# One-core decoder kernel: another order for the first batch of its quantized MLP

## The chip, the cores and the metric

The kernel runs on one core of one Trainium2 chip. The metric is the device time of one execution in microseconds. The median of three runs of the kernel before is 1719.95 us (1714.42 to 1724.76). One execution was profiled: it took 1716.46 us, its trace spans 1714.5 us, and every row below is from it.

## The reference, cut to what matters

Two decoder layers act on x of 4 batches x 512 tokens x 512 features. Each layer is self attention, then a second block, then an MLP, each with a layer norm ahead and a residual around it. The change is in the first layer's MLP, two "bit linear" layers with a GELU between:

```python
def bit_linear(x, w, b, dim_in):
    x_norm = simple_rms_norm(x, dim_in)
    x_q = activation_quant(x_norm)                 # round(x * 127 / max|x|), per token
    w_q = weight_quant(w)                          # sign(w) * mean|w|
    return jnp.einsum('bsd,od->bso', x_q, w_q) + b
h = bit_linear(x, w1, b1, DIM)                     # 512 -> 2048
h = jax.nn.gelu(h, approximate=False)
return bit_linear(h, w2, b2, INNER)                # 2048 -> 512
...
x = x + _L0_xattn_ref(_layernorm(x), ...)          # four experts, a token goes to one
x = x + _L0_ffn_ref(_layernorm(x), w1, b1, w2, b2)
x = x + _L1_attn_ref(_layernorm(x), ...)
```

## The kernel before, in words

The program is a row of phases: Start, Attention, Experts, BitMlp, Attention, Attention (cross), Fp8Linear. Each engine runs its own list in order, and a barrier of all five (L154) stands between phases. SP issues the plain DMAs, POOL (GpSimd) the indirect ones.

Experts writes its results, sorted by expert, to `sorted_y` in memory. BitMlp fetches them: POOL issues one indirect DMA (`take_back`, L145) for each tile of 128 tokens, and the DMA adds into `x`. The four tiles of batch 0 have a semaphore each, `gathered_first`; the later batches one each, `gathered`, with all four tiles on it.

BitMlp works on 4 batches of T = 4 tiles. `steps` runs one step for each tile on each engine: batch 0 unrolled with `first=True`, batches 1 and 2 as a loop, batch 3 unrolled, then four steps that drain the pipeline. `has(k)` says whether the tile k steps back exists. What the engines do:

- VectorE (DVE), `dve_step`. It empties the four PSUM banks of a tile's first layer with scale and bias (L2212, "eviction", 4 instructions). For the tile one step back it takes the row maximum of the GELU's result (L2219) and makes the sum-of-squares operand (L2221). POOL raises that to -1/2 (L2285), and five small operations (`row_factors`, L2146 to L2153) give the tile's factors. Once a batch it also prepares the next batch's input: moments (`norm.dve_moments`, L183 to L194), application (L201), row maxima and squares (`dve_input_rows`, L2162 to L2167), and the input factors (`dve_input_factors`, L2146 to L2153 on four columns) behind a power on POOL (L2278).
- ScalarE (ACT), `act_step`. It applies the GELU (L2119), sums the squares (L2122), scales and rounds the tile one step back (L2127), copies turned tiles out of PSUM (L2089), and at step 2 scales the next batch's four input tiles (L2098).
- TensorE (PE), `pe_step`. It multiplies the first layer (L2053, 16 matmuls a tile), turns the tile three steps back (L2061), multiplies the second layer (L2071), and in step 3, in the midst of those, turns the next batch's input (L2034).

Batch 0 has no batch ahead of it in which to prepare its own input. So `dve` starts with `dve_first_moments` (L2179 to L2189) and `dve_first_factors` (L2194 to L2153) for each of its tiles, with a power on POOL between them (L2310). `act` scales each tile (L2098) and copies it once turned (L2089). `pe` turns tile 0, and inside step 0, behind tile 0's matmuls, it turns tiles 1, 2 and 3 (L2034) ahead of step 1:

```python
        if first and i == 0:
            for k in range(1, T):
                self.pe_first_turn(pe, k)
```

The biases `b1` (1024 KB, the same row for every partition) and `b2` (256 KB) are loaded by SP in `BitMlp.sp`, behind the four `gathered_first` waits. DVE waits for them ahead of its first step.

Of the kernel before, what the change touches and what calls it, by code (L numbers as in the profile page):

```python
# [14 lines left out]
P = 128  # L15
NB = 4
S = 512
D = 512
# [1727 lines left out]
class Experts(Phase):  # L1746
# [15 lines left out]
    def __init__(self, m, name, mats, bufs, early):  # L1762
# [5 lines left out]
        self.xs, self.gate, self.a, self.ys = pair(), pair(), pair(), pair()  # L1768
        self.ahl = take(4 * D, F16).rearrange("p (n a d) -> p n a d", n=2, a=2)
        assert m.used <= ARENA - C * INNER  # L1770
        s = self.sem
# [71 lines left out]
    def sp(self, sp):  # L1843
        self.steps(self.sp_step, sp)
        for k in range(2):
            sp.wait_ge(*self.at(self.sign_done[k], SIGN_PARTS))
            sp.wait_ge(*self.at(self.abs_done[k], SIGN_PARTS))
        self.sp_following(sp)

# [90 lines left out]
class BitMlp(Phase):  # L1940
# [15 lines left out]
    def __init__(self, m, name):  # L1956
        super().__init__(m, name)
        take = m.take
        self.b1, self.b2 = take(INNER), take(D)
        self.h = take(4 * INNER).rearrange("p (n f) -> p n f", n=4)  # L1960
# [10 lines left out]
        self.squares, self.roots = (take(2 * T).rearrange("p (t k) -> p t k", k=2) for _ in range(2))  # L1971
        self.averager = self.junk[:, 0:P]
        assert m.used <= ARENA - C * INNER
        self.signs = m.signs
# [24 lines left out]
    def sp(self, sp):  # L1999
        io, m = self.io, self.m  # L2000
        row = lambda a, n: a.rearrange("(a n) -> a n", a=1).broadcast_to([P, n])

        for t in range(T):
            sp.wait_ge(m.gathered_first[t], 16)
        sp.dma_start(self.b1, row(io["L0_ffn_b1"], INNER)).then_inc(self.const, 16)
        sp.dma_start(self.b2, row(io["L0_ffn_b2"], D)).then_inc(self.const, 16)
        m.wait_back(sp, 1)
        sp.wait_ge(*self.at(self.const, 32))
        self.sp_following(sp)
        self.following.weights.sp_rest(sp)  # L2010

    def steps(self, step, eng):
# [91 lines left out]
    def act_first_turn(self, act, i):  # L2104
        m = self.m
        act.wait_ge(*self.at(self.first_full, i + 1))
        self.act_whole(act, m.xt[:, 0, :, i * P:(i + 1) * P], tile3(m.ps[:, 4 + i, 0:256].bitcast(F16))).then_inc(self.first_free, 1)

    def act_step(self, act, b, i, has, first=False, last=False):
        m = self.m  # L2110
        tile = b * T + i
        if has(3):
            for k in range(2):
                act.wait_ge(*self.at(self.t_full[k], tile - 3 + 1))
                self.act_whole(act, self.q2t[:, (i - 3) % 2, k * 1024:(k + 1) * 1024], m.ps[:, 4 + k, :].bitcast(F16)).then_inc(self.t_free[k], 1)
        if has(0):
            h = self.h[:, i, :]
            act.wait_ge(*self.at(self.bank_free[3], b * (T + 1) + 1 + i))
            act.activation(h, h, ACT.Gelu).then_inc(self.gelu_done, 1)  # L2119
            act.wait_ge(*self.at(self.gelu_done, tile + 1))  # L2120
            act.wait_ge(*self.at(self.ss_done, tile))
            act.activation(self.junk, h, ACT.Square, accum_out=self.ms[:, T + i:T + i + 1]).then_inc(self.ss_done, 1)  # L2122
        if has(1):
            k = (i - 1) % T
            h = self.h[:, k, :]
            act.wait_ge(*self.at(self.factor_chain, tile * self.FACTOR))
            act.activation(h, h, ACT.Identity, scale=self.f[:, T + k:T + k + 1], bias=self.magic).then_inc(self.scaled, 1)  # L2127
        if has(0) and i == 2 and not last:
            self.act_scale_input(act, b + 1)
        if isinstance(b, int) and b == NB and i < self.following.weights.ahead:  # L2130

            self.following.weights.act(act, i)

    def act(self, act):
        act.wait_ge(*self.at(self.consts, 3))
        self.act_first_scale(act, 0)
        for i in range(1, T):
            self.act_first_scale(act, i)
            self.act_first_turn(act, i - 1)
        self.act_first_turn(act, T - 1)  # L2140
        self.steps(self.act_step, act)
# [49 lines left out]
    def dve_first_factors(self, v, ch, i):  # L2191
# [6 lines left out]
        self.row_factors(v, ch, c, D, 0, self.roots[:, i, 1:2], self.alpha1, self.first_factors)  # L2198

    def dve_step(self, v, b, i, has, first=False, last=False):  # L2200
        m = self.m
        tile = b * T + i
        nx = lambda i: slot(m.x, (b + 1) % NB * T + i)
        if has(0):

            for n in range(4):
                v.wait_ge(*self.at(self.bank_full[n], b * (T + 1) + 1 + i))
                if n == 0 and i == 0 and not first:
                    v.wait_ge(*self.at(self.alpha1_ready, b))
                if n == 0 and not first:  # L2210
                    v.wait_ge(*self.at(self.t_full[1], tile - T + 1))
                v.scalar_tensor_tensor(out=self.h[:, i, n * 512:(n + 1) * 512], in0=m.ps[:, n, :], scalar=self.alpha1[:, i:i + 1],  # L2212
                                       in1=self.b1[:, n * 512:(n + 1) * 512], op0=ALU.mult, op1=ALU.add).then_inc(self.bank_free[n], 1)
        if has(1):
# [6 lines left out]
            v.tensor_scalar(self.f[:, col], self.ms[:, col], 1.0 / INNER, 1e-6, ALU.mult, ALU.add).then_inc(self.power2, 1)  # L2221
        if has(0) and i == (1 if first else 0):
            if first:
                m.wait_back(v, 1)
            else:
                m.wait_back(v, 2, 3)
            self.norm.dve_moments(v, b, nx)
# [7 lines left out]
        if has(1):  # L2235
# [3 lines left out]
            ch1.close()  # L2239
        if has(0) and i == 1:  # L2240
            self.norm.dve_apply(v, b, nx, lambda i: m.xn[:, i, :])
            if not last:
                v.wait_ge(*self.at(self.norm.xn_ready, b * T + T))
                self.chi = Chain(self, self.input_chain, self.INPUT, b)
                self.dve_input_rows(v, self.chi, b + 1)
        if has(0) and i == 2 and not last:
            self.dve_input_factors(v, self.chi, b + 1)
# [9 lines left out]
    def dve(self, v):  # L2257
        m = self.m
        ch = Chain(self, self.first_chain, T * self.FIRST, 0)
        self.dve_first_moments(v, ch, 0)  # L2260
        self.dve_first_moments(v, ch, 1)
        v.wait_ge(*self.at(self.abs_all, 1))
        v.tensor_reduce(self.negmean, m.ps[:, 0, 0:2 * SIGN_PARTS].rearrange("p (a n) -> p a n", a=2), AX.X, ALU.add).then_inc(self.mean_done, 1)
        v.wait_ge(*self.at(self.mean_done, 1))
        self.dve_first_factors(v, ch, 0)
        self.dve_first_moments(v, ch, 2)
        self.dve_first_factors(v, ch, 1)
        self.dve_first_moments(v, ch, 3)
        self.dve_first_factors(v, ch, 2)
        self.dve_first_factors(v, ch, 3)  # L2270
        ch.close()
        v.wait_ge(*self.at(self.first_factors, T))
        v.wait_ge(*self.at(self.const, 32))
        self.steps(self.dve_step, v)
# [5 lines left out]
    def pool_step(self, g, b, i, has, first=False, last=False):  # L2280
# [5 lines left out]
        if has(0):  # L2286
            if i == (1 if first else 0):
                self.norm.pool(g, b)
            if i == 1:
                if not last:  # L2290
                    self.pool_root1(g, b + 1)
            xs = slot(m.x, b * T + i)
# [329 lines left out]
```

## Time and profile before

| what | value |
|---|---|
| median of three runs | 1719.95 us |
| the profiled execution | 1716.46 us |
| span of its trace | 1714.5 us |
| TensorE clock granted, mean over the span | 0.958 |
| TensorE matmuls, busy over the span | 1489.2 us (87%) |
| VectorE | 1261.1 us (74%) |
| ScalarE | 871.7 us (51%) |
| GpSimd | 530.4 us (31%) |
| BitMlp, first instruction behind its barrier | 650.79 us |
| next phase, first instruction | 850.90 us |

How to read it: the shares are means over seven phases with different limits, so they say little about BitMlp, which takes 200 us of the 1714.5. There the order of the instructions on each engine and the idle time ahead of single instructions count. The mean clock is close to full speed; single stretches are at half speed.

### The profile page before, as it was taken

The page shows a single profiled execution, that of the slowest core. Times are in us where ns is not written, and L with a number is a line of the kernel's source. Part 1 is how long each engine was busy: PE and PEld are TensorE (multiplying, and loading weights), DVE is VectorE, ACT ScalarE, POOL GpSimd, SP SyncE. Part 2 cuts the span into 40 slices and gives each one's busy share as a digit, 9 for nine tenths or more (in the row PEclk, how much of TensorE's full clock was granted, in tenths as well). Part 3 has the DMA queues.
Part 4 walks back from the last instruction along what each step waited for, and adds up shares of the span by engine and source line. Part 5 has one row for each costly group of instructions (what it writes and reads, how often), then busy time and mean ns, then how long its engine had stood idle before and what let it go on. Part 6 is the DMA issues. An engine that isn't in the chain of part 4 may idle for free. (4 is left out here: it accounts for less than half of the span.)

```text
span 1714.5 us, 26624 instructions
## 1 busy us (share of the span) xinstructions
PE 1489.2 (87%) x8760; PEld 577.9 (34%) x8761; DVE 1261.1 (74%) x1783; ACT 871.7 (51%) x1071; POOL 530.4 (31%) x450
## 2 busy tenths in 40 slices
PE   3789999999959994688798999999999999999948
PEld 1223323233236661344332323333242323323213
DVE  4687897878855556888687788788945776768675
ACT  2245273452822333788737455463837454563735
POOL 1625447355420004422141322323131321414130
PEclk9889999999979997899998999999999999999979
DMA  5241202103313446300230201212031120303002
GB/s 196 74 122 32 68 25 52 47 0 75 119 54 111 147 135 137 54 1 0 62 74 1 54 22 31 84 65 65 25 91 33 45 53 24 73 0 92 12 0 99
DMA packets 82776, 105.40 MB, mean 61 GB/s; under 512 B 14096, under 2 KB 56208, under 8 KB 82576
## 3 DMA queue, kind: packets, MB, share of 16 engines
q1 hardware_dynamic: 79120, 96.10, 19.3%
q0 software_dynamic: 3584, 8.39, 2.3%
q8 instruction: 39, 0.64, 0.2%
q14 instruction: 33, 0.27, 0.1%
HBM read 48.21 MB, written 18.35 MB: 39 GB/s over the span
## 5 line engine op out<-in xcount | busy, mean ns | idle before, releaser
L1224 ACT ACTIVATE arena<-ps 128x1024 f32<-128x1024 f32 x384 | 373.4, 1026 | 108.4 <-PE ps L1075 98.0
L1284 DVE TENSOR_REDUCE arena<-ps 128x2 f32<-128x1024 f32 x256 | 299.7, 1220 | 56.2 <-PE ps L828 56.0
L468 PE MATMUL ps<-xt,w 128*128 128x512 f16 (+1 forms) x1872 | 295.3, 308 | 7.6 <-DVE w L456 3.8
L1075 PE MATMUL ps<-arena 97*128 97x512 f16 (+1 forms) x768 | 211.8, 389 | 14.8 <-ACT arena L1224 10.6
L883 PE MATMUL ps<-arena 128*32 128x512 f32 x1536 | 208.5, 615 | 15.3 <-DVE arena L1319 8.7
L468 PEld LDWEIGHTS ps<-xt,w 128*128 128x128 f16 (+1 forms) x1872 | 151.4, 99 | 141.7 <-issue 36.5
L468 PE MATMUL ps<-w,arena 128*128 128x512 f16 (+1 forms) x804 | 185.5, 381 | 12.7 <-issue 12.7
L1468 DVE TENSOR_TENSOR arena<-arena 128x1024 f32<-128x1024 f32 x128 | 175.2, 1408 | 11.8 <-PE ps L897 9.9
L1725 POOL TENSOR_TENSOR arena<-arena 128x512 f16<-128x512 f32 x96 | 116.6, 1216 | 158.3 <-ACT arena L1204 148.4
L1199 ACT ACTIVATE arena<-ps,arena 128x512 f32<-128x512 f32 x96 | 65.9, 687 | 182.2 <-PE ps L468 171.9
L1581 DVE TENSOR_SCALAR arena<-arena 128x1024 f32<-128x1024 f32 x128 | 106.7, 839 | 68.4 <-ACT arena L1224 67.9
L897 PE MATMUL ps<-arena 128*32 128x512 f32 x1024 | 138.0, 610 | 12.6 <-DVE arena L1468 11.8
L1595 POOL TENSOR_TENSOR arena<-arena 128x512 f16<-128x512 f32 x36 | 56.4, 1566 | 276.5 <-ACT arena L1145 276.5
L1075 PEld LDWEIGHTS ps<-arena 97*128 97x128 f16 (+1 forms) x768 | 59.2, 98 | 198.2 <-issue 100.9
L468 PEld LDWEIGHTS ps<-w,arena 128*128 128x128 f16 x804 | 75.7, 98 | 108.6 <-issue 30.5
L1135 ACT ACTIVATE arena<-ps 128x512 f32<-128x512 f32 x48 | 28.7, 597 | 136.7 <-PE ps L468 136.7
L468 PE MATMUL ps<-w,xt 128*128 128x512 f16 x384 | 92.0, 380 | 0.0
L828 PE MATMUL ps<-arena 32*128 32x512 f16 x512 | 70.0, 394 | 23.9 <-DVE arena L1284 21.7
L2071 PE MATMUL ps<-arena 128*128 128x512 f16 x256 | 63.3, 401 | 27.7 <-ACT arena L2089 27.7
L201 DVE TENSOR_SCALAR xn<-x,mv,rstd 128x512 f32 (+1 forms) x76 | 63.6, 890 | 24.4 <-POOL rstd L214 24.4
L2053 PE MATMUL ps<-arena,xt 128*128 128x512 f16 x256 | 61.9, 399 | 14.1 <-DVE arena L2212 9.4
L211 POOL TENSOR_TENSOR rstd<-mv,eps 128x4 f32<-128x4 f32 x27 | 9.8, 363 | 189.1 <-DVE mv L194 180.1
(217 smaller groups left out, 2001.5 us busy)
## 6 DMA issues: line engine op xcount, KB each, us to landing
arena<-arena SPq DMA_DIRECT2D x576, 64.0 KB, 2.0
raw<-in_ffn_parts SPq DMA_DIRECT2D x16, 512.0 KB, 3.8
raw<-in_ctxT SPq DMA_DIRECT2D x7, 1024.0 KB, 5.2
sorted_x<-arena SPq DMA_DIRECT2D x1, 4864.0 KB, 17.2
arena<-sorted_x SPq DMA_DIRECT2D x19, 256.0 KB, 3.7
sorted_y<-arena SPq DMA_DIRECT2D x19, 256.0 KB, 2.1
out<-x SPq DMA_DIRECT2D x16, 256.0 KB, 2.0
x<-in_x SPq DMA_DIRECT2D x1, 3072.0 KB, 12.0
```

Source lines behind the costliest of these rows:

```text
L201: v.tensor_scalar(dst(i), src(i), m.mv[:, i, 0:1], m.rstd[:, i:i + 1], ALU.subtract, ALU.mult).then_inc(self.xn_ready, 1)
L468: last = pe.matmul(out, left[l](cl[k]), right[r](cr[k]), start=start and k == 0 and a == 0, stop=stop and k == n - 1 and a == 2)
L828: last = pe.matmul(banks[:, k, :], self.qf[rows, 1, 0, g, t * P:(t + 1) * P], self.qf[rows, 0, 0, g, :], start=True, stop=True, tile_posit ...
L883: last = pe.matmul(self.context(g)[HD * j:HD * (j + 1)], self.v[:, kb, HD * (HG * g + j):HD * (HG * g + j + 1)], self.p(u)[:, j * S:(j + 1 ...
L897: last = pe.matmul(self.m.ps[HD * j:HD * (j + 1), 7, :], self.ones, p[:, j * S:(j + 1) * S], start=start, stop=stop, tile_position=(0, HD ...
L1075: last = pe.matmul(self.m.ps[:, j4, :], self.kst[0:R, HG * g + j4, kb * P:(kb + 1) * P], self.qst[0:R, HG * g + j4, :], start=True, stop=True)
L1199: act.activation(self.qb[:, n % 2, :], self.bank(item), ACT.Identity, scale=s, bias=self.pb[:, C * w + c:C * w + c + 1]).then_inc(self.ban ...
L1224: act.activation(self.p(u)[:, 2 * h * S:(2 * h + 2) * S], flat(self.m.ps[:, 2 * h:2 * h + 2, :]), ACT.Exp, scale=SOFTMAX_SCALE).then_inc(s ...
L1284: v.tensor_reduce(self.mx[:, g % 2, j:j + 2, t:t + 1].rearrange("p h t -> p (h t)"), self.slot_banks(item, b), AX.X, ALU.max).then_inc(sel ...
L1468: v.tensor_tensor(self.pair_sum[:, cols], self.p(2 * n)[:, cols], self.p(2 * n + 1)[:, cols], ALU.add).then_inc(self.paired, 1)
L1581: v.tensor_scalar(p, p, slot_col(self.hi, b * T + kb), CLIP_LOW, ALU.min, ALU.max).then_inc(self.clipped[h], 1)
L1725: g.tensor_tensor(self.qf[:, w, 1, c, :], src[:, n % 2, :], self.qf[:, w, 0, c, :], ALU.subtract).then_inc(self.fl, 1)
```

## The change

Four things are altered, all in batch 0 of BitMlp.

1. The loads of `b1` and `b2` move from `BitMlp.sp` to `sp_early`, which SP runs at the end of the Experts phase, behind its last store and ahead of its waits for the signs. The buffers move to the end of BitMlp's space, where Experts has nothing.
2. VectorE's opening is reordered. Tile 0's factors come ahead of tile 1's moments, and tile 0's eviction comes ahead of tile 3's factors. The wait for all four `first_factors` moves behind that eviction.
3. In step 1 the moments of batch 1 come behind tile 0's factors, and the application and the input rows move to step 2, behind tile 1's factors, with the input factors right behind them. POOL's power for them moves to step 2 as well.
4. ScalarE's opening is reordered: scale 0, copy 0, scale 1, scale 2, copy 1, GELU of tile 0, scale 3, copy 2, copy 3. TensorE's list stays as it is.

```diff
@@ Experts.sp
         self.steps(self.sp_step, sp)
+        self.sp_following(sp)
         for k in range(2):
             sp.wait_ge(*self.at(self.sign_done[k], SIGN_PARTS))
             sp.wait_ge(*self.at(self.abs_done[k], SIGN_PARTS))
-        self.sp_following(sp)
@@ BitMlp.sp, sp_early
-        for t in range(T):
-            sp.wait_ge(m.gathered_first[t], 16)
-        sp.dma_start(self.b1, row(io["L0_ffn_b1"], INNER)).then_inc(self.const, 16)
-        sp.dma_start(self.b2, row(io["L0_ffn_b2"], D)).then_inc(self.const, 16)
         m.wait_back(sp, 1)
...
+    def sp_early(self, sp):
+        row = lambda a, n: a.rearrange("(a n) -> a n", a=1).broadcast_to([P, n])
+        sp.dma_start(self.b1, row(self.io["L0_ffn_b1"], INNER)).then_inc(self.const, 16)
+        sp.dma_start(self.b2, row(self.io["L0_ffn_b2"], D)).then_inc(self.const, 16)
@@ act_step
-            act.wait_ge(*self.at(self.bank_free[3], b * (T + 1) + 1 + i))
-            act.activation(h, h, ACT.Gelu).then_inc(self.gelu_done, 1)
+            if not (first and i == 0):
+                self.act_gelu(act, b, i)
@@ act
         self.act_first_scale(act, 0)
-        for i in range(1, T):
-            self.act_first_scale(act, i)
-            self.act_first_turn(act, i - 1)
-        self.act_first_turn(act, T - 1)
+        self.act_first_turn(act, 0)
+        self.act_first_scale(act, 1)
+        self.act_first_scale(act, 2)
+        self.act_first_turn(act, 1)
+        self.act_gelu(act, 0, 0)
+        self.act_first_scale(act, 3)
+        self.act_first_turn(act, 2)
+        self.act_first_turn(act, 3)
@@ dve_step
-        if has(0):
-            for n in range(4):
...
+        if has(0) and not (first and i == 0):
+            self.dve_first_layer(v, b, i, first)
@@ dve_step, between the maximum and the factors of the tile one step back
-        if has(0) and i == (1 if first else 0):
-            if first:
-                m.wait_back(v, 1)
-            else:
-                m.wait_back(v, 2, 3)
+        if has(0) and i == 0 and not first:
+            m.wait_back(v, 2, 3)
             self.norm.dve_moments(v, b, nx)
@@ dve_step, behind those factors
-        if has(0) and i == 1:
+        if first and i == 1:
+            m.wait_back(v, 1)
+            self.norm.dve_moments(v, b, nx)
+        if has(0) and i == (2 if first else 1):
             self.norm.dve_apply(v, b, nx, lambda i: m.xn[:, i, :])
@@ dve
         self.dve_first_moments(v, ch, 0)
-        self.dve_first_moments(v, ch, 1)
...
         self.dve_first_factors(v, ch, 0)
+        self.dve_first_moments(v, ch, 1)
         self.dve_first_moments(v, ch, 2)
         self.dve_first_factors(v, ch, 1)
         self.dve_first_moments(v, ch, 3)
         self.dve_first_factors(v, ch, 2)
+        v.wait_ge(*self.at(self.first_factors, 1))
+        v.wait_ge(*self.at(self.const, 32))
+        self.dve_first_layer(v, 0, 0, True)
         self.dve_first_factors(v, ch, 3)
@@ pool_step
-            if i == 1:
-                if not last:
-                    self.pool_root1(g, b + 1)
+            if i == (2 if first else 1) and not last:
+                self.pool_root1(g, b + 1)
```

## Rows read from the trace of the kernel before

**Rows 1.** Busy time in two stretches: us, PE, PEld, DVE, ACT, POOL, PEclk, DMA.
```profile
656.48:701.71 45.23, 20.71 (x96) 9.11 (x96) 36.75 (x101) 22.47 (x20) 26.80 (x23) 0.70 0.64 139
713.96:754.88 40.92, 34.38 (x209) 18.05 (x208) 36.34 (x75) 34.48 (x28) 9.52 (x11) 0.96 0.05 7
```

**Rows 2.** Who waited for whom, BitMlp: us in total, times, longest us.
```profile
PE ps L2053 <- DVE arena L2212: 9.4, 1, 9.4
```

**Rows 3.** Timeline, tile 0: start us, us, engine, line, [idle before <-releaser].
```profile
656.48 0.69 DVE L2179 BATCH_NORM_STATS2 stats<-x 128x6 f32<-128x512 f32 x1 [10.26 <-DMA x<-sorted_y,place]
658.12 0.73 POOL L2310 TENSOR_TENSOR arena<-arena,mhalf 128x2 f32<-128x2 f32 x1 [3.01 <-DVE arena L2189]
...
660.51 0.55 DVE L2194 TENSOR_SCALAR xn<-x,mv,arena 128x512 f32<-128x512 f32 x1
...
662.80 0.81 ACT L2098 ACTIVATE arena<-xn,arena 128x512 f32<-128x512 f32 x1 [14.32 <-DVE arena L2153]
...
668.23 0.67 ACT L2089 ACTIVATE xt<-ps,arena 128x512 f16<-128x512 f16 x1
...
668.95 5.81 PE L2053 MATMUL ps<-arena,xt 128*128 128x512 f16 x16 [4.68 <-ACT xt L2089]
```

**Rows 4.** Timeline, fetches of tiles 2 and 3.
```profile
659.04 1.57 POOL L145 DMA_INDIRECT x<-sorted_y,place  x1 [0.19 <-issue]
...
661.80 1.60 POOL L145 DMA_INDIRECT x<-sorted_y,place  x1 [0.17 <-issue]
...
663.82 0.69 DVE L2179 BATCH_NORM_STATS2 stats<-x 128x6 f32<-128x512 f32 x1 [1.14 <-DMA x<-sorted_y,place]
```

**Rows 5.** Timeline, first evictions and matmuls of tiles 1 and 2; matmuls after a pause.
```profile
674.16 2.73 DVE L2212 SCALAR_TENSOR_TENSOR arena<-ps,arena 128x512 f32<-128x512 f32 x4 [1.09 <-DMA arena<-in_L_ffn_b]
...
676.70 7.07 PE L2053 MATMUL ps<-arena,xt 128*128 128x512 f16 x32
...
677.77 3.34 DVE L2212 SCALAR_TENSOR_TENSOR arena<-ps,arena 128x512 f32<-128x512 f32 x4 [0.88 <-PE ps L2053]
...
747.62 2.75 PE L2071 MATMUL ps<-arena 128*128 128x512 f16 x8 [3.97 <-ACT arena L2089]
```

**Rows 6.** Timeline, three ScalarE table loads, one with what follows it.
```profile
677.61 1.28 ACT L2119 ACT_TABLE_LOAD   x1
...
507.84 1.28 ACT L1899 ACT_TABLE_LOAD   x1
...
513.23 0.60 ACT L1899 ACTIVATE arena<-ps 128x512 f32<-128x512 f32 x1 [4.10 <-PE ps L468]
...
900.51 1.28 ACT L1224 ACT_TABLE_LOAD   x1 [3.17 <-PE ps L1075]
```

**Rows 7.** Timeline, preparation of batch 1 on VectorE and GpSimd.
```profile
681.03 2.28 DVE L2219 TENSOR_REDUCE arena<-arena 128x1 f32<-128x2048 f32 x1
683.28 2.46 DVE L183 BATCH_NORM_STATS2 stats<-x 128x6 f32<-128x512 f32 x4
...
685.88 0.28 DVE L194 BATCH_NORM_AGGREGATE mv<-stats 128x2 f32<-128x6 f32 x3
...
687.64 1.92 DVE L201 TENSOR_SCALAR xn<-x,mv,rstd 128x512 f32<-128x512 f32 x4 [0.74 <-POOL rstd L214]
...
692.26 2.72 DVE L2212 SCALAR_TENSOR_TENSOR arena<-ps,arena 128x512 f32<-128x512 f32 x4
692.43 1.01 POOL L2278 TENSOR_TENSOR arena<-arena,mhalf 128x4 f32<-128x4 f32 x1 [4.90 <-DVE arena L2167]
```

**Rows 8.** Timeline, tile 1's factors and batch 1's input factors.
```profile
698.94 0.16 DVE L2146 SCALAR_TENSOR_TENSOR arena<-arena 128x1 f32<-128x1 f32 x1 [1.71 <-POOL arena L2285]
...
699.88 1.26 POOL L2296 TENSOR_TENSOR x<-x,arena 128x512 f32<-128x512 f32 x1 [0.97 <-DVE arena L2153]
699.90 1.26 DVE L2148 TENSOR_SCALAR arena<-arena 128x4 f32<-128x4 f32 x1
...
701.54 0.17 DVE L2153 SCALAR_TENSOR_TENSOR arena<-arena 128x4 f32<-128x4 f32 x1
```

More of the change, by code:

```diff
@@ L1769, in __init__ @@
         self.ahl = take(4 * D, F16).rearrange("p (n a d) -> p n a d", n=2, a=2)
+        m.experts_used = m.used
         assert m.used <= ARENA - C * INNER
@@ L1958, in __init__ @@
         take = m.take
-        self.b1, self.b2 = take(INNER), take(D)
         self.h = take(4 * INNER).rearrange("p (n f) -> p n f", n=4)
@@ L1972, in __init__ @@
         self.averager = self.junk[:, 0:P]
+        assert m.used >= m.experts_used
+        self.b1, self.b2 = take(INNER), take(D)
         assert m.used <= ARENA - C * INNER
@@ L2000, in sp @@
         io, m = self.io, self.m
-        row = lambda a, n: a.rearrange("(a n) -> a n", a=1).broadcast_to([P, n])
-        for t in range(T):
-            sp.wait_ge(m.gathered_first[t], 16)
-        sp.dma_start(self.b1, row(io["L0_ffn_b1"], INNER)).then_inc(self.const, 16)
-        sp.dma_start(self.b2, row(io["L0_ffn_b2"], D)).then_inc(self.const, 16)
         m.wait_back(sp, 1)
@@ L2107, in act_first_turn, with act_gelu @@
         self.act_whole(act, m.xt[:, 0, :, i * P:(i + 1) * P], tile3(m.ps[:, 4 + i, 0:256].bitcast(F16))).then_inc(self.first_free, 1)
+    def act_gelu(self, act, b, i):
+        h = self.h[:, i, :]
+        act.wait_ge(*self.at(self.bank_free[3], b * (T + 1) + 1 + i))
+        act.activation(h, h, ACT.Gelu).then_inc(self.gelu_done, 1)
     def act_step(self, act, b, i, has, first=False, last=False):
@@ L2127, in act_step @@
             act.activation(h, h, ACT.Identity, scale=self.f[:, T + k:T + k + 1], bias=self.magic).then_inc(self.scaled, 1)
-        if has(0) and i == 2 and not last:
+        if has(0) and i == (2 if first else 2) and not last:
             self.act_scale_input(act, b + 1)
@@ L2198, in dve_first_factors, with dve_first_layer @@
         self.row_factors(v, ch, c, D, 0, self.roots[:, i, 1:2], self.alpha1, self.first_factors)
+    def dve_first_layer(self, v, b, i, first):
+        m, tile = self.m, b * T + i
+        for n in range(4):
+            v.wait_ge(*self.at(self.bank_full[n], b * (T + 1) + 1 + i))
+            if n == 0 and i == 0 and not first:
+                v.wait_ge(*self.at(self.alpha1_ready, b))
+            if n == 0 and not first:
+                v.wait_ge(*self.at(self.t_full[1], tile - T + 1))
+            v.scalar_tensor_tensor(out=self.h[:, i, n * 512:(n + 1) * 512], in0=m.ps[:, n, :], scalar=self.alpha1[:, i:i + 1],
+                                   in1=self.b1[:, n * 512:(n + 1) * 512], op0=ALU.mult, op1=ALU.add).then_inc(self.bank_free[n], 1)
     def dve_step(self, v, b, i, has, first=False, last=False):
@@ L2203, in dve_step @@
         nx = lambda i: slot(m.x, (b + 1) % NB * T + i)
-        if has(0):
-            for n in range(4):
[L2207 to L2213, printed above, removed]
+        if has(0) and not (first and i == 0):
+            self.dve_first_layer(v, b, i, first)
         if has(1):
@@ L2245, in dve_step @@
                 self.dve_input_rows(v, self.chi, b + 1)
-        if has(0) and i == 2 and not last:
+        if has(0) and i == (2 if first else 2) and not last:
             self.dve_input_factors(v, self.chi, b + 1)
@@ L2272, in dve @@
         v.wait_ge(*self.at(self.first_factors, T))
-        v.wait_ge(*self.at(self.const, 32))
         self.steps(self.dve_step, v)
```

## The prediction

> **What bounds the kernel now.** The change touches only BitMlp, so I first compared two stretches of it by busy time [rows 1]. From one batch's first eviction to the next one's is 40.92 us, and VectorE is busy in 36.34 of them, ScalarE and TensorE in less. VectorE's list sets the pace there, and those batches are left as they are. The other stretch is the opening, from the first moments at 656.48 to the end of batch 1's input factors at 701.71. VectorE is busy in 36.75 of its 45.23 us, so 8.48 us are idle. Next I looked at the waits: TensorE sits 9.4 us for one eviction, tile 2's [rows 2], which VectorE reaches at 692.26 behind the whole norm of batch 1 [rows 7]. That wait looks like the prize. It isn't, unless the instant at which batch 1 can start moves with it. Last I followed the timeline [rows 3 to 8] to that instant. ScalarE scales batch 1's input only when the input factors are done, and its next copies, TensorE's second layer, the turn of batch 1 and batch 1's first matmuls all stand behind that scaling. I call the end of the input factors the gate: 701.54 + 0.17 = 701.71 [rows 8]. By then the evictions of tiles 0 to 2, the factors of tiles 0 and 1 and the whole input of batch 1 are done. In the new order exactly the same work lies ahead of the gate, so the change is worth what the gate moves. It can't gain more than VectorE's idle time of 8.48 us ahead of it, which is just under 0.5% of 1716.46. It can lose without such a limit.
>
> **Opening, tile 0.** Its moments take 656.48 to 658.0 and POOL's power 658.12 to 658.85 [rows 3]. Today tile 1's moments lie between, and the factors start at 660.51. From there to ScalarE's start at 662.80 is 2.3 us, 2.2 of it VectorE's. Moved ahead, they run from 658.95 to 661.1, and VectorE idles 0.7 us for the power. ScalarE scales until 662.05, TensorE turns (0.6), ScalarE copies in 0.67 [rows 3], and tile 0's matmuls start at 663.5, not 668.95: 5.4 us earlier. At the pace of today's row (5.81 us) they end at 669.3. Alone this gains nothing, since VectorE isn't there to evict.
>
> **The fetch of tile 3.** POOL's power for tile 1 now waits for moments that end at 661.1 + 1.55 = 662.65, and POOL's next fetch is queued behind it. The power ends at 663.5 and the fetch starts 0.2 later, at 663.7, not 661.80. A fetch lands 4.8 us behind its start (659.04 to 663.82) [rows 4], so tile 3 is there at 668.5. VectorE has finished tile 2's moments (663.82 + 1.55) and tile 1's factors (2.2) at 667.5 and idles 1.0. Tile 3's moments end at 670.05, tile 2's factors at 672.2. On POOL the two fetches of batch 1 that follow stay where they are, since they were behind tile 2's power.
>
> **Biases.** Tile 0's eviction waited 1.09 us for b1 [rows 5]. With the loads ahead of the barrier that wait goes: eviction 672.3 to 675.0, 1.9 us earlier than today's 674.16 + 2.73. I cost the two loads at nothing in Experts: SP issues them behind its last store, and POOL's first fetch moves no data until well over 1 us behind the barrier. Bounds: below nothing if the fetches run faster without them beside (0.3), and above by the 4.8 of one landing if they held up the first fetch. I take 0, because they are issued before the barrier opens.
>
> **Tile 1's matmuls.** This is the step that costs. TensorE turns tiles 1, 2 and 3 ahead of step 1, and tile 3 needs its scaling, which needs its factors. Those stand behind tile 0's eviction on VectorE: 675.05 to 677.2. On ScalarE the scaling stands behind the GELU as well. That waits for the eviction, until 675.05, and needs a table load of 1.28 us. The load at 507.84 came 5.4 us ahead of its own activation at 513.23, which waited for TensorE, so a load can run under the wait [rows 6]. ScalarE is free from 673.9, so the load ends at 675.2 and the GELU (1.9) at 677.1, just as the factors do. Scaling ends at 678.1, the turn at 678.75, and tile 1's matmuls start at 678.8, today 676.70: 2.1 later. Today they find TensorE at full speed, 7.07 us for two tiles or 3.5 each [rows 5]. In the new order it has done two turns of 0.6 us in the 8.9 us since tile 0. Today 8 matmuls behind a pause of 3.97 us take 2.75 us [rows 5], 0.34 each, near tile 0's 5.81 / 16 = 0.36 and far from 3.5 / 16 = 0.22. So I take tile 0's pace, 5.7 us, with the first four at the lower of the two clock levels, 1.2 GHz, where 512 columns take 0.43 us. The last bank is full at 684.5 and evicted by 685.3; today 677.77 + 3.34 = 681.1. VectorE idles 3.4 us ahead of the first bank and 2.0 between the banks. At full speed tile 1's eviction would end at 683.1.
>
> **Step 1.** Maximum and sum 2.45 [rows 7], to 687.75. Then VectorE idles 0.8 for POOL's power. Today the moments lie under this wait. Factors 0.8 (698.94 to the next chain) [rows 8], to 689.35. Moments of batch 1, 683.28 to 686.16 [rows 7], 2.9, to 692.25. Tile 2's eviction then starts where it does today, at 692.26. All that was saved is gone by here, and today batch 1's normalized input is complete by then.
>
> **Step 2.** Eviction 2.72, to 695.0. Maximum and sum to 697.4. POOL's power stands behind tile 1's bias add and two fetches, as today, where VectorE idles 1.71 and goes on at 698.94 [rows 8]. POOL reaches them 0.2 later, so factors from 699.15 to 700.0. Application and input rows 687.64 to 692.35, 4.7 [rows 7], to 704.7. POOL's power 0.1 + 1.01 [rows 7], to 705.8; today it lies under tile 2's eviction, now VectorE waits for it. Input factors: today 1.9 to 2.0, of which one operation took 1.26 beside POOL's bias add [rows 8]. POOL's next instruction behind the power is again such an add, so I take 2.0; without the collision it is 0.9. The gate is at 707.8, range 706.7 to 707.8, today 701.71: **6.1 us later**.
>
> The same by idle time: the new order leaves VectorE 0.7, 1.1, 1.0, 3.4, 2.0, 0.8, 1.7 and 1.1, in sum 11.8 us, where today's waits were 0.8, 1.1, 1.1, 0.9, 0.6, 0.7 and 1.7, in sum 6.9. These give 4.9; the rest is rounding and the small gaps between dependent operations.
>
> Behind the gate both lists are the same, the lead of tile 0 has been used up, and each batch repeats one period, so I carry the 6.1 to the end.
>
> **A rule of the skill.** Here the table load at 677.61 was followed at once by its activation, and nothing beside its 1.28 us was paid. The Trainium skill, ScalarE: Activation LUTs, What ACT_TABLE_LOAD costs, adds a drain of about 1.38 us to each switch. By that rule the GELU ends 1.4 later and the change loses about 7.5 us. The sum above goes by the row.
>
> **Rivals.** A, the load runs behind the wait: at 900.51 a load came only at the end of an idle time of 3.17 us [rows 6]. Then the GELU ends 1.1 later, scaling and tile 1 with it: +7.2. The order of load and wait decides; the case is within my forecast's range. B, TensorE is at full speed for tile 1: the eviction ends at 683.1, gate at 705.6, +3.9. The turns at 673.3 and 678.2 speak for it, the slow matmuls behind 3.97 us of pause against. C, the change does what it is meant to. The turn of tile 3 doesn't hold tile 1 (its scaling ends by 674.5), so tile 1 is evicted right behind tile 3's factors, 677.2 to 679.95. Then 2.45 + 0.8 + 0.8 + 2.9 for step 1 give 686.9, and 2.7 + 2.45 + 0.8 + 0.8 + 4.7 + 1.1 + 0.9 for step 2 give 700.4: 1.3 us faster. TensorE's list, with three turns ahead of step 1, speaks against it. D, the later batches swallow the delay: VectorE has 4.6 us idle in each [rows 1]. Then 0. Against it: the idle stands at the turn of the batches, inside the chain that starts at the gate. E, the losses add: A, and a first fetch held up by b1's 1 MB for a few us: +9 to +12.
>
> **How the numbers follow.** Forecast with A: +5 to +7.5, chance 0.60. B 0.16, C 0.06, D 0.09, E 0.09. The profiled execution, 1716.46, is 3.5 us below the median, 1719.95. 1716.46 + 6.1 = 1722.6 there, and 1726 on the median. The runs before lie within 5 us of their median, so I give 1717 to 1732: from C to the foot of E, with some of that spread. 0.5% is 8.6 us, about what a measurement of this kernel can tell from no change. The forecast lies below that bound, but 2.5 us more, by E or by the spread, crosses it: slower 0.23. Faster by 8.6 would take all of the idle time: 0.04. The same 0.73.
>
> **What the profile would show.** Tile 0's matmuls at about 663.5; a wait for the fetch of tile 3; no wait for b1; the turn of tile 3 at 678 behind a pause of TensorE; tile 1's matmuls at tile 0's pace; VectorE idle for L2285 twice and for L2278 once; input factors ending at 707.8; the period between batches still 40.9 us. The prediction is wrong if tile 1's matmuls start before 676, or if the end moves otherwise than the gate.

## The result and the profile after

The changed kernel takes 1723.4 us in the median of 20 runs (1716.54 to 1730.38), the kernel before 1716.44 us (20 runs, 1713.13 to 1724.76). The ratio is 1.0039, 95% interval 1.0027 to 1.0050: by the ratio slower by 6.7 us, with 4.6 and 8.6 as its ends (the two medians lie 7.0 apart). That is 0.39%, so it stayed within the 0.5% that the prediction set as the bound to slower, with a chance of 0.73 for staying there. Twenty runs of each tell it from no change all the same. The forecast was 6.1 us slower. Its 1726 stood on the first three runs of before, whose median lay 3.5 us above that of the twenty.

The profiled execution of the changed kernel took 1723.83 us, span 1721.7. Its BitMlp begins 3.8 us later than that of before (654.62 against 650.79), so all that follows is counted from BitMlp's first moments: 656.48 in the kernel before, 660.38 here. Line numbers have moved: L2055 is the first layer (before L2053), L2220 the eviction (L2212), L2158 to L2165 the factors (L2146 to L2153), L2304 and L2297 POOL's powers (L2285, L2278), L2100 the scaling (L2098), L2091 the copy (L2089), L2036 the turn (L2034), L2114 the GELU (L2119), L2206 the first application (L2194), L2191 the first moments (L2179). In the kernels of the experiments the same lines are off by a few again.

Busy time of the changed kernel in two stretches, the opening up to the gate and one batch, with the columns of [rows 1]:

```profile
660.38:710.66 50.28, 23.37 (x96) 10.03 (x96) 36.74 (x101) 22.76 (x20) 26.80 (x23) 0.70 0.50 98
723.14:764.05 40.91, 34.38 (x209) 18.06 (x208) 36.34 (x76) 34.47 (x28) 9.51 (x11) 0.96 0.05 7
```

This is the case in two lines. VectorE is busy for 36.74 us ahead of the gate (the end of batch 1's input factors), 36.75 before, in the same 101 instructions; the stretch is 50.28 us long, not 45.23. All of the 5.05 us is idle time. The later batches are as they were: 40.91 us from eviction to eviction, 36.34 of them busy.

Who waited for whom, where [rows 2] had 9.4 us:

```profile
PE ps L2055 <- DVE arena L2220: 4.7, 1, 4.7
```

TensorE's longest wait in the opening has halved, and the kernel is slower.

The opening of the changed kernel, from its timeline (start us, us, engine, line):

```profile
662.85 0.55 DVE L2206 TENSOR_SCALAR xn<-x,mv,arena 128x512 f32<-128x512 f32 x1 [0.84 <-POOL arena L2328]
...
667.37 6.22 PE L2055 MATMUL ps<-arena,xt 128*128 128x512 f16 x16 [0.78 <-ACT xt L2091]
667.45 1.60 POOL L145 DMA_INDIRECT x<-sorted_y,place  x1 [0.19 <-issue]
...
672.49 0.69 DVE L2191 BATCH_NORM_STATS2 stats<-x 128x6 f32<-128x512 f32 x1 [1.12 <-DMA x<-sorted_y,place]
...
676.10 2.73 DVE L2220 SCALAR_TENSOR_TENSOR arena<-ps,arena 128x512 f32<-128x512 f32 x4
...
677.58 1.28 ACT L2114 ACT_TABLE_LOAD   x1
...
678.88 1.91 ACT L2114 ACTIVATE arena<-arena 128x2048 f32<-128x2048 f32 x1
...
680.92 0.81 ACT L2100 ACTIVATE arena<-xn,arena 128x512 f32<-128x512 f32 x1
...
681.79 0.61 PE L2036 MATMUL ps<-ident,arena 128*128 128x128 f16 x4 [4.13 <-ACT arena L2100]
682.19 9.11 PE L2055 MATMUL ps<-arena,xt 128*128 128x512 f16 x32
...
684.22 0.75 DVE L2220 SCALAR_TENSOR_TENSOR arena<-ps,arena 128x512 f32<-128x512 f32 x1 [3.34 <-PE ps L2055]
...
685.85 0.75 DVE L2220 SCALAR_TENSOR_TENSOR arena<-ps,arena 128x512 f32<-128x512 f32 x1 [0.88 <-PE ps L2055]
687.02 1.61 DVE L2220 SCALAR_TENSOR_TENSOR arena<-ps,arena 128x512 f32<-128x512 f32 x2 [0.42 <-PE ps L2055]
```

Tile 0's matmuls start 6.99 us behind the first moments (12.47 before), and its eviction at 15.72 without a wait for b1 (17.68 before). Then TensorE pauses 4.13 us for the scaling of tile 3, turns that tile, and only then starts tile 1, at 21.81 (20.22 before). VectorE waits 3.34 us for the first bank and ends the eviction at 28.25 (24.63 before).

The clock at tile 1, changed kernel first, then the kernel before (same columns):

```profile
682.19:685.70 3.51, 3.51 (x11) 1.31 (x10) 0.75 (x1) 2.69 (x4) 3.05 (x3) 0.50 0.54 166
```

```profile
677.00:684.00 7.00, 6.77 (x32) 2.86 (x30) 5.89 (x8) 6.94 (x6) 2.56 (x3) 1.00 0.98 202
```

The granted clock is 0.50 against 1.00: 1.2 GHz, where the kernel before ran tiles 1 and 2 at 2.4 GHz. The clock rises later within the tile: its sixteen matmuls take 5.66 us at a mean of 0.64.

Steps 1 and 2 of the changed kernel:

```profile
691.58 0.16 DVE L2158 SCALAR_TENSOR_TENSOR arena<-arena 128x1 f32<-128x1 f32 x1 [0.69 <-POOL arena L2304]
...
695.15 2.69 DVE L2220 SCALAR_TENSOR_TENSOR arena<-ps,arena 128x512 f32<-128x512 f32 x4
...
702.11 0.16 DVE L2158 SCALAR_TENSOR_TENSOR arena<-arena 128x1 f32<-128x1 f32 x1 [2.02 <-POOL arena L2304]
...
708.66 1.25 POOL L2314 TENSOR_TENSOR x<-x,arena 128x512 f32<-128x512 f32 x1
708.72 1.22 DVE L2158 SCALAR_TENSOR_TENSOR arena<-arena 128x4 f32<-128x4 f32 x1 [1.12 <-POOL arena L2297]
...
710.50 0.16 DVE L2165 SCALAR_TENSOR_TENSOR arena<-arena 128x4 f32<-128x4 f32 x1
```

VectorE waits for all three powers of POOL in these steps (tile 0's, tile 1's and that of batch 1's input), 0.69, 2.02 and 1.12 us. Tile 2's eviction starts at 34.77, a little earlier than before (35.78), but the gate comes at 50.28, not 45.23. One operation of the input factors takes 1.22 us beside POOL's bias add, as one did before [rows 8].

### The profile page after: what moved, and what is told of

The parts are those of the page before. It is cut to its first block and busy times, and to the rows that moved or that the text cites. A ratio compares the mean times of both kernels' runs of the same rounds, so it can differ in the third digit from the quotient of the medians.

```text
span 1721.7 us, 26623 instructions
## 1 busy us (share of the span) xinstructions
PE 1494.3 (87%) x8760; PEld 579.1 (34%) x8761; DVE 1260.6 (73%) x1783; ACT 871.3 (51%) x1071; POOL 530.8 (31%) x450
## 5 line engine op out<-in xcount | busy, mean ns | idle before, releaser
L2055 PE MATMUL ps<-arena,xt 128*128 128x512 f16 x256 | 64.0, 409 | 5.5 <-DVE arena L2220 4.7
```

What stands on the lines that cost most here:

```text
L2055: ended = pe.matmul(m.ps[:, n, :], m.xt[:, 0, c, i * P:(i + 1) * P], sg[:, c * INNER + n * 512:c * INNER + (n + 1) * 512], start=c == 0, s ...
```

## The experiments

Each kernel was profiled once and timed in alternation with the kernel before. The second to fourth columns are counted from BitMlp's first moments: the end of tile 1's eviction, the gate, and the start of batch 1's first matmul. Then come the sixteen matmuls of a second layer near the end of BitMlp, behind a pause of 3.3 us, which have a part in what follows, the length of BitMlp (its first instruction to the next phase's first), and the measured ratio.

| kernel | tile 1 evicted | gate | batch 1 begins | 16 behind the pause | BitMlp | ratio, 95% |
|---|---|---|---|---|---|---|
| before | 24.63 | 45.23 | 56.21 | 5.12 | 200.11 | |
| before, again (`e8`) | 24.76 | 45.34 | 56.32 | 5.13 | 200.24 | 0.9992 (0.9976 to 1.0007) |
| early loads alone (`e1`) | 25.48 | 46.06 | 57.46 | 3.61 | 199.04 | 0.9998 (0.9986 to 1.0010) |
| norm alone (`e2`) | 24.31 | 46.34 | 56.32 | 6.35 | 201.54 | 1.0023 (1.0010 to 1.0036) |
| loads and opening (`e3`) | 28.46 | 49.03 | 59.45 | 6.50 | 205.02 | 1.0038 (1.0023 to 1.0054) |
| changed | 28.25 | 50.28 | 61.49 | 5.29 | 205.60 | 1.0039 (1.0027 to 1.0050) |
| changed, turn of tile 3 late (`e4`) | 23.29 | 45.32 | 56.25 | 5.14 | 200.26 | 1.0008 (0.9996 to 1.0020) |
| changed, scaling of tile 3 first (`e5`) | 25.56 | 47.60 | 58.86 | 5.30 | 203.03 | 1.0015 (1.0003 to 1.0026) |
| `e3`, turn late (`e6`) | 23.42 | 44.00 | 54.18 | 6.36 | 199.43 | 1.0007 (0.9990 to 1.0025) |
| `e6`, fetches behind the power (`e7`) | 23.13 | 41.60 | 52.89 | 6.36 | 198.20 | 1.0007 (0.9985 to 1.0028) |
| the same again (`e10`) | 23.30 | 41.78 | 53.09 | 5.00 | 197.17 | 0.9995 (0.9981 to 1.0009) |
| before, fetches behind the power (`e9`) | 24.01 | 42.50 | 54.78 | 5.21 | 199.00 | 1.0007 (0.9991 to 1.0023) |

The gate less the end of tile 1's eviction shows what each order costs VectorE between the two: 20.57 to 20.60 us in the five traces with the norm where it was, 22.03 or 22.04 in the four with the norm moved, and 18.47 to 18.49 in the three with the fetches moved. So the moved norm costs 1.45 us, and what is left of a difference between gates arose at tile 1 or ahead of it: 3.62 + 1.45 = 5.07 for the changed kernel, against 5.05.

**The loads alone.** The changed kernel with the lists of VectorE, ScalarE and POOL set back. What is left of the change, cut:

```diff
@@ BitMlp.sp
-    sp.dma_start(self.b1, ...)
-    sp.dma_start(self.b2, ...)
@@ BitMlp.sp_early
+    sp.dma_start(self.b1, ...)
+    sp.dma_start(self.b2, ...)
```

> Part 1 alone: b1 and b2 are loaded at the end of Experts, all else as in the kernel before. I count from the first moments of BitMlp to the end of batch 1's input factors, the gate: 45.23 us in the kernel before, 50.28 in the changed one. My theory (the time follows the gate, and the gate follows VectorE's idle time): the wait of 1.1 us for b1 goes, but tile 1's matmuls started at 20.2 us because of ScalarE's copies, not because of that wait, so tile 1's eviction and the gate stay within 0.3 us, ratio 1.000. Rival U (the 3.8 us by which BitMlp began later in the changed kernel's trace come from these loads beside the last store of Experts): the opening barrier of BitMlp is late again by 3 to 4 us against before, ratio 1.002, which would be most of the loss of 6.7.

The time is that of before, so the rival falls. BitMlp began at 656.29 in this trace, but it began at 654.85 in the second trace of before, without the loads, and at 651.52 and 650.70 in two kernels with them (`e3`, `e4`). The start varies by itself: its mean is 653.97 in the four traces without the early loads and 653.93 in the eight with them. The gate came 0.8 us late, outside my 0.3: TensorE ran nearly all of tile 0 at the low clock here (granted clock 0.54, before 0.62),

```profile
674.98 6.59 PE L2055 MATMUL ps<-arena,xt 128*128 128x512 f16 x16 [4.92 <-ACT xt L2091]
```

6.59 us where [rows 3] has 5.81. Tile 0's matmuls ended 0.86 us later (19.14 against 18.28), and tile 1's started as much later (21.08 against 20.22). The wait for b1 had hidden nothing worth having: tile 1 stood behind TensorE and ScalarE anyway. BitMlp is 1.1 us shorter all the same; the sixteen matmuls behind the pause, 1.5 us faster here, have to do with no load.

**The norm alone.** The kernel before with part 3:

```diff
-        if has(0) and i == (1 if first else 0):      # moments ahead of tile 0's factors
+        if first and i == 1:                          # moments behind them
...
-        if has(0) and i == 1:                         # application, input rows
+        if has(0) and i == (2 if first else 1):
```

> Part 3 alone: batch 1's moments behind tile 0's factors, application and input rows in step 2, the opening as before. Theory: tile 1's eviction ends at 24.6 us as before; then 2.45 + 0.8 idle + 0.8 + 2.9 to tile 2's eviction (31.6 us, before 35.8), and in step 2 VectorE idles for the power of tile 1 and for that of the input, so that the gate comes at 47.1 us, 1.9 later than before; ratio 1.001. TensorE's wait for tile 2's eviction shrinks from 9.4 us to about 5 all the same. Rival C (TensorE's wait is what costs): the gate or the end comes earlier by up to 4 us, ratio 0.998.

```profile
687.22 0.16 DVE L2146 SCALAR_TENSOR_TENSOR arena<-arena 128x1 f32<-128x1 f32 x1 [0.69 <-POOL arena L2286]
...
691.65 5.97 PE L2053 MATMUL ps<-arena,xt 128*128 128x512 f16 x16 [4.71 <-DVE arena L2212]
...
697.75 0.16 DVE L2146 SCALAR_TENSOR_TENSOR arena<-arena 128x1 f32<-128x1 f32 x1 [2.02 <-POOL arena L2286]
...
704.36 1.22 DVE L2146 SCALAR_TENSOR_TENSOR arena<-arena 128x4 f32<-128x4 f32 x1 [1.12 <-POOL arena L2279]
```

TensorE's wait is 4.71 us and not 9.4, as in the changed kernel, tile 2 is evicted 5 us earlier (30.82 to 35.78), and the gate still comes 1.1 us later. The rival called C in this expectation, that TensorE's wait is what costs, falls. The three waits for POOL are here too. Of the 1.9 us expected 1.1 came: tile 1's eviction ended 0.3 earlier than before, and step 1 took 6.51 us, not 6.95. What the later gate did to the end this trace doesn't show. Batch 1's first matmul came at 56.32, as in the kernel before, because TensorE ran faster between the gate and it: it turned batch 1's input in 1.05 us, where the trace of before has 1.88. The order doesn't explain that: the other three traces with the norm moved have 1.89 to 1.92. BitMlp is 1.4 us longer, but the sixteen matmuls behind the pause alone took 1.2 more. The ratio says 3.9 us (1.7 to 6.2), more than the gate's 1.1; that difference stays open.

**The loads and the opening, with the norm put back.**

```diff
-        if first and i == 1:
+        if has(0) and i == (1 if first else 0):
...
-        if has(0) and i == (2 if first else 1):
+        if has(0) and i == 1:
```

> Parts 1, 2 and 4: the changed kernel with batch 1's norm put back where it was. Theory: tile 1's eviction ends at 28.3 us as in the changed kernel (before 24.6), the two powers are covered again, the gate comes at about 49.2 us, 4.0 later than before and 1.1 earlier than in the changed kernel; ratio 1.0023. If the loss is the norm's instead, the gate is back at 45.2 and the ratio is 1.000.

```profile
681.31 0.75 DVE L2220 SCALAR_TENSOR_TENSOR arena<-ps,arena 128x512 f32<-128x512 f32 x1 [3.34 <-PE ps L2055]
...
703.77 0.16 DVE L2158 SCALAR_TENSOR_TENSOR arena<-arena 128x1 f32<-128x1 f32 x1 [1.70 <-POOL arena L2303]
```

VectorE waits 3.34 us for tile 1's first bank, as in the changed kernel, and the gate is at 49.03: 3.8 later than before, 1.25 earlier than in the changed kernel. The two parts add: 3.8 + 1.1 = 4.9, against 5.05 for both. BitMlp is 4.9 us longer, of which 1.4 are the sixteen matmuls behind the pause (6.50 against 5.12).

**The turn of tile 3 behind tile 1's matmuls**, all else as changed:

```diff
         if first and i == 0:
-            for k in range(1, T):
+            for k in range(1, T - 1):
                 self.pe_first_turn(pe, k)
+        if first and i == 1:
+            self.pe_first_turn(pe, T - 1)
```

> The changed kernel, but TensorE turns tile 3 behind tile 1's matmuls instead of ahead of them. Theory: what holds tile 1's matmuls is the turn of tile 3, which waits for the scaling behind the eviction and the GELU. Without it they start at about 17.3 us instead of 21.8, tile 1's eviction follows tile 3's factors and ends at about 23.7 instead of 28.3, and the gate comes at about 45.8 instead of 50.3: ratio 1.0003 against before. Rival K (TensorE's low clock and ScalarE's order hold tile 1, not the turn): the eviction ends at 27 or later, ratio 1.003 or more.

```profile
673.75 5.16 PE L2055 MATMUL ps<-arena,xt 128*128 128x512 f16 x16 [0.18 <-ACT xt L2093]
...
677.06 2.73 DVE L2222 SCALAR_TENSOR_TENSOR arena<-ps,arena 128x512 f32<-128x512 f32 x4
...
678.75 0.39 PE L2036 MATMUL ps<-ident,arena 128*128 128x128 f16 x4
```

Tile 1's matmuls start at 17.25, its eviction follows tile 3's factors without a wait, and the gate is at 45.32: 5.0 us come back. This names the cause of what tile 1 lost. The low clock alone doesn't cost: these matmuls took 5.16 us at a mean clock of 0.70, not 3.62 at 1.00 as before, but under VectorE's work. Rival K falls.

**Tile 3's factors and scaling ahead of tile 0's eviction and GELU.**

```diff
-        self.dve_first_layer(v, 0, 0, True)
         self.dve_first_factors(v, ch, 3)
+        self.dve_first_layer(v, 0, 0, True)
...
-        self.act_gelu(act, 0, 0)
         self.act_first_scale(act, 3)
         self.act_first_turn(act, 2)
         self.act_first_turn(act, 3)
+        self.act_gelu(act, 0, 0)
```

> The changed kernel, but tile 3's factors stand ahead of tile 0's eviction on VectorE, and tile 3's scaling and the copies of tiles 2 and 3 ahead of the GELU on ScalarE. Theory (the turn of tile 3 holds tile 1's matmuls, wherever its delay comes from): scaling at 18.0 us behind the first moments, turn at 18.9, tile 1's matmuls at about 19.6 instead of 21.8, its eviction ends at about 26.0 instead of 28.3, the gate comes at about 48.0 instead of 50.3; ratio 1.0016 against before. Rival: if it is the eviction of tile 0 that counts and not the turn, moving it back makes things worse than the changed kernel, gate over 50.3.

```profile
678.46 0.61 PE L2036 MATMUL ps<-ident,arena 128*128 128x128 f16 x4 [1.50 <-ACT arena L2100]
...
680.88 0.75 DVE L2220 SCALAR_TENSOR_TENSOR arena<-ps,arena 128x512 f32<-128x512 f32 x1 [0.69 <-PE ps L2055]
```

The turn comes at 18.6 and tile 1's matmuls at 19.01, 2.8 us earlier, and the gate at 47.60, 2.7 earlier than in the changed kernel. The same turn, freed from its other side, gives the same kind of gain. So what holds tile 1 through that turn is tile 0's work put ahead of the last scaling: its eviction on VectorE and its GELU on ScalarE. Which of the two held it isn't separated, since this run moves both; in the changed kernel the scaling starts at 680.92, behind a GELU that ends at 680.79 and factors that end at 680.89.

**The late turn with the norm put back.** The kernel with the loads and the opening alone, and the edit of the late turn.

> TensorE's late turn of tile 3 and the norm of batch 1 where it was before, with the changed kernel's loads and opening. Theory (idle times of VectorE add): tile 1's eviction ends at 23.3 us as with the late turn alone, and from there to the gate it takes the 20.6 us of the kernel with the opening alone: gate at 43.9, 1.3 earlier than in the kernel before; ratio 0.9992. If the two parts don't add, the gate is at 45 or later.

The gate is at 44.00 where 43.9 was expected; batch 1's first matmul comes 2.0 us earlier than before, but BitMlp is only 0.7 us shorter, since the sixteen matmuls behind the pause took 6.36 us against 5.12. Of POOL's three powers in steps 1 and 2 only tile 1's still holds VectorE for long, as in the kernel before:

```profile
702.04 0.16 DVE L2160 SCALAR_TENSOR_TENSOR arena<-arena 128x1 f32<-128x1 f32 x1 [1.71 <-POOL arena L2305]
```

**The fetches behind the power.**

```diff
 # pool_step, behind the power for the tile one step back
+            if first and i == 2:
+                m.take_back(g, 2, (2, 3))
...
-            if first:
+            if first and i != 1:
                 m.take_back(g, 2 + i // 2, (2 * (i % 2), 2 * (i % 2) + 1))
```

> As the kernel before this one in the list, and in addition POOL issues the two fetches of step 1 behind the power for tile 1's factors instead of ahead of it. Theory: VectorE's wait of about 1.7 us for that power falls to 0.7 or less, gate at about 42.5, 2.7 earlier than in the kernel before; ratio 0.998. Rival: the fetches of batches 2 and 3 that are now later hold up batch 2's moments, which wait for them, and the gain is given back in batch 1: the gate is early, but batch 1's norm begins later.

```profile
702.00 0.16 DVE L2160 SCALAR_TENSOR_TENSOR arena<-arena 128x1 f32<-128x1 f32 x1 [0.67 <-POOL arena L2305]
...
702.96 2.08 ACT L2136 ACTIVATE arena<-arena 128x2048 f32<-128x2048 f32 x1
...
703.53 0.16 DVE L2167 SCALAR_TENSOR_TENSOR arena<-arena 128x4 f32<-128x4 f32 x1
...
704.94 2.91 ACT L2102 ACTIVATE arena<-xn,arena 128x512 f32<-128x512 f32 x4
...
711.12 0.16 DVE L2160 SCALAR_TENSOR_TENSOR arena<-arena 128x1 f32<-128x1 f32 x1 [2.40 <-POOL arena L2305]
```

The wait falls to 0.67. The bias add no longer lies beside the input factors either, which I had not counted on, and the gate comes at 41.60, not 42.5: 2.4 us earlier than in the kernel ahead of this one in the table (`e6`). But batch 1's first matmul gains only 1.3 of it, and BitMlp 1.2; the sixteen matmuls behind the pause took 6.36 us in both. The gate opens at 703.69, and ScalarE is still scaling tile 1 until 705.04: the gate has stopped being the last thing to come. The ratio, 1.0007, is not the 0.998 that was expected. The fetches that were moved now stand ahead of the next tile's power, where VectorE waits 2.40 us; that wait lies beside TensorE's second layer. Batch 2's moments weren't held up (VectorE doesn't wait ahead of them, and they come 1.3 us earlier than in `e6`), so the rival fell.

**The kernel before, again.**

> The kernel before, unchanged, for the spread of a single trace and of the ratio: gate at 45.2 us within 0.9, BitMlp 200.1 us within 1.5, ratio 1.000. If both vary by more than that, differences of 1 us between the other traces tell nothing.

Gate 0.11 and BitMlp 0.13 us from the first trace. The other kernel with two traces (`e7`, `e10`) has gates 0.18 and BitMlp 1.03 us apart. So a difference of 1 us between gates can be read, with the time of tile 0's matmuls beside it as for the early loads; one of 1 us between lengths of BitMlp can't.

**The fetches behind the power in the kernel before.**

> The kernel before with one edit: POOL issues the two fetches of step 1 behind the power for tile 1's factors. Theory: VectorE's wait of 1.7 us for that power falls to 0.7, and the bias add no longer lies beside the input factors, so the gate comes 2.3 us earlier, at about 42.9 us. But ScalarE then scales tile 1 (2.1 us) when the gate opens, so only 1.4 us of it arrive: BitMlp at about 198.8 instead of 200.1; ratio 0.9992. If the gate alone set the end, BitMlp would take 197.8.

Gate 42.50, BitMlp 199.00, as expected, since ScalarE's scaling of tile 1 ends 1.3 us behind the gate here too. The ratio doesn't show it.

**The best of these again.**

> The kernel with early loads, reordered opening, late turn of tile 3, norm where it was and fetches behind the power, again with more rounds: BitMlp 198.2 us as in its first trace within 1.0, gate 41.6 within 0.9, ratio 0.999 if the 1.9 us of BitMlp are what the time sees. If the ratio is 1.001 or more, the order costs something outside BitMlp.

BitMlp 197.17, a hair outside the 1.0 allowed for it, and gate 41.78. The ratio is 0.9995, its interval 0.9981 to 1.0009. Against the kernel before BitMlp is shorter by 1.9 and 2.9 us in two traces (their sixteen matmuls behind the pause took 6.36 and 5.00 us), but no gain in time is shown.

## Why the prediction was right

**The bound.** The gate was the right place to look, and what hangs on it can be followed further. Batch 1's first matmul comes 10.0 to 11.4 us behind the gate in the nine traces without the moved fetches. The spread goes with TensorE's clock: the turn of batch 1's input takes 1.05 us in the trace with 10.0, and 1.86 to 1.92 in the six with 10.9 to 11.4. In the three with the moved fetches it comes 11.3 to 12.3 us behind, because ScalarE's scaling starts 1.25 us behind the gate. From batch 1's first matmul to the end, less the sixteen matmuls behind the pause, it is 133.0 to 133.1 us in eleven of the twelve traces. In the twelfth, the early loads alone, it is 131.8, and there batch 3 began 39.3 us behind batch 2, not 40.9. So behind the gate the orders are alike, as predicted, and what differs, but for that scaling, is TensorE's clock, by up to 1.4 us ahead of batch 1 and by up to 2.9 us at that pause. First the kernel before, then the early loads:

```profile
834.17 5.12 PE L2071 MATMUL ps<-arena 128*128 128x512 f16 x16 [3.32 <-ACT arena L2089]
```

```profile
839.67 3.61 PE L2073 MATMUL ps<-arena 128*128 128x512 f16 x16 [3.32 <-ACT arena L2091]
```

The granted clock is 0.70 over the first, 1.00 over the second.

**Tile 0 and the fetch of tile 3.** Matmuls predicted at 7.0 behind the first moments (663.5), measured 6.99. The fetch was predicted 7.2 behind them, measured 7.07; VectorE was to wait 1.0 for it and waited 1.12.

**Tile 1.** Start predicted at 22.3, measured 21.81; eviction's end at 28.8, measured 28.25. VectorE's waits were to be 3.4 and 2.0 and were 3.34 and 1.3. The sixteen matmuls were to take 5.7 us and took 5.66. The table load ran under the wait for the eviction: it starts at 677.58, during the eviction of 676.10 to 678.83, and the GELU follows at 678.88. So rival A, a load behind the wait, didn't happen, and no drain was paid behind the load. Rival B, full clock at tile 1, is refuted by the granted 0.50 in its first 3.5 us.

**Step 1.** From tile 1's eviction to tile 2's I had 6.95 us, measured 6.52. The pieces were each rounded up a little: VectorE's instructions begin some 0.05 to 0.1 before the one ahead has ended, and POOL's power cost 0.69, not 0.8.

**Step 2.** From tile 2's eviction to the gate I had 15.55, measured 15.51, with the waits for tile 1's power (2.02; I had 1.7) and the input's power (1.12; I had 1.1), and the collision with the bias add.

**The sum.** The gate moved by 5.05 to 50.28, predicted 6.1; that is still inside the prediction's range for it, 706.7 to 707.8 or 50.2 to 51.3 behind the first moments. The start of tile 1's matmuls and step 1 were each put about half a microsecond too late or too long. The prediction had a second count, by VectorE's idle time: 11.8 us against 6.9, which gives 4.9, and it put the rest down to rounding and small gaps. The waits measured are 11.7 against 7.0. VectorE was as busy as before, so that count was the better one, and the 6.1 was about 1 us too high. BitMlp is longer by 5.5 us: 5.05 at the gate, 0.2 on TensorE between the gate and batch 1's first matmul, 0.2 at the pause and 0.1 ahead of the first moments. The time is longer by 6.7 (4.6 to 8.6); 5.5 lies inside. What the other 1.2 us are, if they are real, stays open, so it is partly luck that 6.1 lies as near to 6.7 as it does. The trace can't settle it. Stretches that the change doesn't touch differ between traces by more: from the end of BitMlp to the end of the span it is 860.6 to 865.5 us over the twelve traces, 863.6 in that of before and 861.5 in that of the changed kernel.

**Rivals C and D.** C needed the turn of tile 3 out of the way. With it out of the way tile 1's eviction ended at 23.29, where C had 23.5, but the gate came at 45.32, not 1.3 us ahead of before. C's sum for step 2 was too small by 2.1 us: it had 0.8 us for the wait for tile 1's power, which was 2.03, and no collision of the input factors with the bias add, where one operation took 1.22 us. D, that later batches swallow the delay, is refuted by the period of 40.91 us and by BitMlp's length. E's cause, a first fetch held up by b1, didn't occur: from BitMlp's first instruction to the first moments it is 5.76 us in the changed kernel and 5.69 before.

## What to carry to other kernels

Look for the instant behind which everything is the same in both orders, list what must be done ahead of it on the engine that paces the stage, and count that engine's idle time, not another's longest wait: here the longest wait was halved and the kernel got slower. When a step is moved forward, follow what its new place pushes back on every engine that has a fixed order; the turn of tile 3, in a list that nobody edited, used up the 5.5 us by which tile 0's matmuls came earlier, and tile 1 was evicted 3.6 us later than before. Work that stands between a request to another engine and its result is a cover, and moving it behind the result uncovers the wait: 1.45 us here. And before a difference of 1 us between two traces is put down to an edit, look for it in a stretch that the edit can't reach.

## What the runs showed of the hardware that I had not expected

TensorE's clock behind a pause isn't the same from run to run. Near the end of BitMlp all twelve traces have the same sixteen matmuls behind a pause of 3.31 or 3.32 us. They took 3.61 us in one, 5.00 to 5.30 in seven and 6.35 to 6.50 in four. Two traces of one kernel, `e7` and then `e10`, differ as well (columns of [rows 1]):

```profile
836.47:842.83 6.36, 6.36 (x19) 2.37 (x20) 0.00 (x0) 4.64 (x3) 0.00 (x0) 0.56 0.00 0
833.55:838.55 5.00, 5.00 (x19) 2.03 (x20) 0.00 (x0) 4.64 (x3) 0.00 (x0) 0.72 0.00 0
```

In the same two traces tile 0's sixteen matmuls took 6.43 and 5.17 us. This moves a phase by 1 to 2 us with no edit near it: the lengths of BitMlp of `e7` and `e10` differ by 1.03 us. The Trainium skill, TensorE: Matmul & The Clock Gate, What's actually happening, says that the gate passes half of the pulses or all of them, depending on recent activity. These rows agree, with a mean of 1.00 over the fastest sixteen, 0.50 over the first 3.5 us of tile 1 in the changed kernel, and values between where the clock rises on the way.

A GELU's table load starts while its activation waits for another engine, here 1.25 us ahead of the end of what it waited for. The Trainium skill, ScalarE: Activation LUTs, What ACT_TABLE_LOAD costs, adds a drain of about 1.38 us to the load's 1.28. The rows here don't bear that out: they show 1.30 us from the load's start (677.58) to the activation's start (678.88), nothing between the end of the load and it but 0.02 us, and 1.91 us for the activation itself. ScalarE had nothing else to do at the time; whether a drain is paid when it has, no run here shows.
